# Value items of odd units in slots 3, 7 and 11, between the groups of value matmuls, in a two-layer attention kernel

## The reference

```python
Q = (q_in @ wq + bq).reshape(Bq, Sq, H, HD)
Kp = (k_in @ wk + bk).reshape(Bq, Sk, H, HD)
V = (v_in @ wv + bv).reshape(Bq, Sk, H, HD)
scores = jnp.einsum('bqhd,bkhd->bhqk', Q, Kp) / jnp.sqrt(jnp.float32(HD))
a = jax.nn.softmax(scores, axis=-1)
o = jnp.einsum('bhqk,bkhd->bqhd', a, V).reshape(Bq, Sq, Dm)
return o @ wo + bo
```

## Time and profile before

| what | value |
|---|---|
| median of 3 runs | 594.2 us (594.09 to 597.36) |
| profiled execution, its own time | 590.02 us |
| its span, first to last instruction | 588.2 us |
| mean granted TensorE clock | 0.937 |
| TensorE matmul busy | 518.5 us (88%) |
| VectorE busy | 431.1 us (73%) |
| ScalarE busy | 363.8 us (62%) |
| GpSimd busy | 205.7 us (35%) |
| L376, matmuls of the value items | 192 instructions for each layer's weights, 8 for each item |

### The profile page before, as it was taken

One profiled execution on the slowest core, in us unless ns is written; L12 is line 12 of the kernel. 1 busy time (PEld: TensorE's weight loads), 2 busy tenths in 40 slices (PEclk: granted clock), 3 DMA queues, 4 the chain that ended last, 5 costly groups with the idle time before them and its releaser, 6 DMA issues.

```text
span 588.2 us, 17011 instructions
## 1 busy us (share of the span) xinstructions
PE 518.5 (88%) x6536; PEld 378.8 (64%) x6536; DVE 431.1 (73%) x818; ACT 363.8 (62%) x716; POOL 205.7 (35%) x357
## 2 busy tenths in 40 slices
PE   6878779999999999998699993899999999999985
PEld 4756357676767767686467772467667676767763
DVE  7799978777777779876361126878989897978753
ACT  2556357777776776777334432476767667676663
POOL 8553123122130337353133002436547373530101
PEclk9789679999999999999869996699999999999998
DMA  6337478657747365465302310357373743528000
GB/s 162 102 116 210 156 194 250 171 183 180 205 144 196 130 193 153 137 183 175 95 2 86 91 37 15 101 157 218 141 185 125 190 151 108 168 69 228 12 3 17
DMA packets 41117, 79.99 MB, mean 136 GB/s; under 512 B 9327, under 2 KB 19247, under 8 KB 41055
## 3 DMA queue, kind: packets, MB, share of 16 engines
q1 hardware_dynamic: 41054, 79.16, 46.7%
HBM read 58.95 MB, written 20.13 MB: 134 GB/s over the span
## 4 chain that ended last, share of the span: by engine, by line
PE 57%; DVE 19%; ACT 8%; issue 8%; POOL 3%; DMA 3%; SPq 1%; ACTq 1%; POOLq 0%; DVEq 0%
PE bank L442 11%; PE bank L420 10%; PE bank L408 9%; PE bank L1302 5%; PE bank L376 4%; PE bank L370 4%; PE bank L1291 4%; DVE mx L609 4%; PE bank L364 3%; DVE qfix L601 2%; ACT qfix L539 2%; DMA k_scratch<-kparts 2%; PE bank L382 2%; ACT scratch L562 2%; DVE weights L1490 1%
## 5 line engine op out<-in xcount | busy, mean ns | idle before, releaser
L609 DVE TENSOR_REDUCE mx<-bank 112x1 f32<-112x500 f32 x384 | 245.3, 673 | 45.8 <-PE bank L408 42.8
L562 ACT ACTIVATE scratch<-bank 125x448 f32<-125x448 f32 x384 | 203.6, 548 | 111.9 <-PE bank L420 110.1
L408 PE MATMUL bank<-krep,qfix 96*112 96x500 bf16 (+1 forms) x384 | 153.6, 410 | 5.3 <-DVE mx L609 2.7
L420 PEld LDWEIGHTS bank<-qfix,krep 99*128 99x128 bf16 (+1 forms) x1536 | 107.6, 101 | 73.3 <-issue 26.0
L420 PE MATMUL bank<-qfix,krep 99*128 99x112 bf16 (+1 forms) x1536 | 140.1, 215 | 15.3 <-ACT qfix L539 10.1
L442 PE MATMUL bank<-scratch,v 125*32 125x112 f32 x3072 | 94.0, 262 | 0.0
L442 PEld LDWEIGHTS bank<-scratch,v 125*32 125x32 f32 x3072 | 70.2, 109 | 9.2 <-ACT scratch L562 0.6
L735 POOL TENSOR_TENSOR oT<-comb,rec 128x56 f32<-128x56 f32 x32 | 10.0, 312 | 175.0 <-DVE rec L631 175.0
L408 PEld LDWEIGHTS bank<-krep,qfix 96*112 96x112 bf16 (+1 forms) x384 | 51.5, 136 | 29.3 <-issue 18.6
L724 POOL TENSOR_TENSOR kparts<-k_rest,kparts 128x500 bf16<-128x500 f32 x48 | 54.3, 1139 | 43.1 <-ACT kparts L546 42.8
L1302 PEld LDWEIGHTS bank<-scratch 128*112 128x112 f32 x256 | 32.7, 182 | 16.0 <-issue 10.7
(11 more groups left out here) (172 smaller groups left out, 706.3 us busy)
## 6 DMA issues: line engine op xcount, KB each, us to landing
krep<-k_scratch SPq DMA_DIRECT2D x192, 187.5 KB, 4.0
k_scratch<-kparts SPq DMA_DIRECT2D x16, 1125.0 KB, 4.5
ctx_tile<-in_ctx SPq DMA_DIRECT2D x16, 750.0 KB
scratch<-in_L_xattn_e_w SPq DMA_DIRECT2D x16, 256.0 KB, 3.1
Q<-q_scratch SPq DMA_DIRECT2D x12, 168.0 KB, 3.1
q_scratch<-scratch SPq DMA_DIRECT2D x6, 168.0 KB, 2.5
Q<-q_scratch SPq DMA_DIRECT2D x12, 56.0 KB, 2.3
k_rest<-in_selq SPq DMA_DIRECT2D x1, 576.0 KB, 11.1
```

The costliest lines, as they stand in the source:

```text
L408: nc.tensor.matmul(row_bank(v, c, lead)[0:PQ, 0:KB], qfix[0:KR[l], slot, p * PQ:(p + 1) * PQ], krep[0:KR[l], slot, p, n * KB:(n + 1) * KB] ...
L420: ins = nc.tensor.matmul(SCORES[c % 2][:, p * PQ:(p + 1) * PQ], krep[0:KS[l], slot, p, c * KP:c * KP + 128], qfix[0:KS[l], slot, p * PQ:(p ...
L562: nc.scalar.activation(P[:, p_slot(s_, slot), :], SCORES[slot % 2][0:KP, 0:UQ], ACT.Exp, scale=SCALE).then_inc(z["exp_ok"], 1)
L609: nc.vector.tensor_reduce(mx[:, par, c // NKB, c % NKB:c % NKB + 1], row_bank(v, c, lead)[0:PQ, 0:KB], AX.X, ALU.max).then_inc(z["row_max" ...
```

## The change

The table of items gives odd units their V items in slots 3, 7 and 11 in place of 1, 5 and 8. As V2 now stands behind M, the list that tells an item which one was two places before it, `before` in `pe_attend`, starts the later passes with M and V2 in that order.

```diff
         STEP_ITEMS = [
...
-            {1: [("V", 1, 0)], 4: [("D", -1)], 5: [("V", 1, 1)], 8: [("V", 1, 2)], 10: [("M", 1)]},
+            {3: [("V", 1, 0)], 4: [("D", -1)], 7: [("V", 1, 1)], 10: [("M", 1)], 11: [("V", 1, 2)]},
...
-            {1: [("V", 2, 0)], 4: [("D", -1)], 5: [("V", 2, 1)], 8: [("V", 2, 2)], 10: [("M", 1)],
+            {3: [("V", 2, 0)], 4: [("D", -1)], 7: [("V", 2, 1)], 10: [("M", 1)], 11: [("V", 2, 2)],
              13: [("D", 0)]},
...
-                before = [("V", 2 * j, 2, 0, l), ("D", -1, 0, 3, l) if begins(j) else ("M", 4 * j, 0, 0, l)]
+                before = [("V", 2 * j, 2, 0, l), ("D", -1, 0, 3, l)] if begins(j) else \
+                    [("M", 4 * j, 0, 0, l), ("V", 2 * j, 2, 0, l)]
```

## The result

| | before | changed |
|---|---|---|
| median of 18 runs each | 593.95 us | 596.75 us |
| ratio to before, 95% interval | | 1.0063 (1.0041 to 1.0084) |
| profiled execution, its own time | 590.02 us | 594.52 us |
| its span | 588.2 us | 592.7 us |

The forecast was 597.2 us on a base of 594.2, +0.5%. The changed kernel is slower by 0.6%, clear of no change in 18 runs, and by less than the 1% that the prediction took as the least that could be told from no change. (The quotient of the two medians alone is 1.0047, inside the interval.)

A forecast was written before the change was run, and what follows sets the result against it. TensorE was taken to bound ordinary odd units, with a blocked VectorE copy lengthening six others. Terms 0.0 + 4.4 - 1.2 - 0.15 summed to +3.0 us, giving 597.2 us on a base of 594.2; range 588.5 to 600.0.

The forecast's parts named there:

- (a): Six ordinary layer 0 odd units followed by T items: M 0.80 us earlier, T1 later behind it, net 0.0.
- (b): Six long odd units: qfix copy still blocked by GpSimd's multiplication, M unmoved, T1 later by 0.73 us each, +4.4.
- (c): Layer 1 units 11 and 13, whose successors have no T items: -0.6 us each, -1.2.
- (d): Last unit of layer 0: V2 fills TensorE's wait for an exponential ahead of the last score matmuls, -0.15 us.
- rival C: Ordinary odd units: GpSimd's five steps gate M, so it comes no earlier; +9.4 us, 603.6 us; chance 0.08.
- Rival A: Long odd units: qfix copy gets in before GpSimd's multiplication, freeing them; sum -4.2 us, 590.0 us; chance 0.27.
- Rival B: Start of even units: T1 doesn't wait for ScalarE's copy of V2; sum +0.4 us, 594.6 us; chance 0.15.

The follow-up runs named there:

- e1: The changed kernel with V2 back in slot 8, ahead of M, V0 and V1 staying in slots 3 and 7; ratio to the kernel before 1.0009.
- e2: The kernel before with only V2 moved, from slot 8 to slot 11 behind M; ratio to the kernel before 1.0102.
- e3: The changed kernel with the three T items of even units one slot later (1, 2, 3); ratio to the kernel before 1.0104.
- e4: The kernel before with VectorE's copy of queries into qfix in slot 4 in place of 5; ratio to the kernel before 0.9892.
- e6: The kernel before with V0 of odd units in slot 0 in place of 1; ratio to the kernel before 0.9785.

## Why the prediction was right

The forecast had the sign, the size (+0.5% against +0.6%) and the mechanism: V2 leaves a place where its 0.87 us cost little, ahead of M, and enters one where nothing hides it. e1 shows that it is V2 and not the other two, and the changed kernel's own rows show where.

By terms, from the lengths between M items in the profiled executions (changed less before):

| term | forecast | measured |
|---|---|---|
| (a) six ordinary units with T behind them | 0.0 | about +1.8: four pairs +0.22 to +0.25, unit 13 and its successor +0.56, unit 1 and its successor +0.27 (+1.43 less the 1.16 by which the transfer's wait grew) |
| (b) six long units | +4.4 | +3.75: five pairs of layer 1 +4.10 together, unit 11 of layer 0 -0.35 |
| (c) two units without T behind them | -1.2 | -0.72 |
| (d) last unit of layer 0 | -0.15 | +0.02 (M of unit 14 to the first M of layer 1) |
| sum | +3.0 | about +4.8 |

The parts that are in no term: 0.15 us up to the M of layer 0's first unit, -1.35 in layer 1's first unit at its other clock, -0.27 behind the last M, and the transfer's 1.16. With them, the span's +4.5 is complete.

That the totals lie so near is in part luck: the ordinary units cost 1.8 us where I had nothing, (c) won 0.5 us less, and the one copy that got in first gave 1.1 us back.

(a) and (c) were mis-sized by one step: "Ahead of M, an ordinary unit gets shorter by 0.87 - 0.07 = 0.80". It measured 0.59 in unit 5 and 0.52 to 0.61 in the others but unit 13 of layer 0. The 0.07 is there in units 5 and 9 (0.50 between the first two score matmuls) and is 0.14 in the others (0.57), and I had not followed the exponentials through the slots that are bare now, so that the score matmuls of slot 9 wait 0.17 us for that of slot 7. e2 shows the same in a purer form. In unit 13 of layer 0 M itself then waits 0.18 us for GpSimd's steps, a trace of rival C, and there the odd unit became only 0.28 shorter. In (d) the wait of 0.15 is gone, but with V2 out of slot 8 the score matmuls at 281.74 and 285.09 wait 0.21 and 0.44 us for exponentials; that unit is 0.19 longer up to its last sums. Behind M the forecast was T1 at M + 3.07, measured 3.06, with 0.05 us more for T1 itself, whose weight load waits with it.

(b) was right in five units, where the even unit grew by 0.77 to 0.86 in place of 0.73, and wrong in the sixth. Rival A was real: the 0.11 to 0.20 us by which I had GpSimd first became 0.10 to 0.12, and in unit 11 of layer 0 the copy won. Freed, this unit's M came 1.19 us earlier, for which rival A had 1.2. Had all six gone so, the measured terms would sum to about -1.0; the starts of the two outcomes lie within 0.02 us.

Rival B (T1 follows without a wait) was wrong: T1 waits the 0.22 us that I had, and e3, which takes this wait away, puts another of the same size behind it. Rival C did not decide ordinary units: but for unit 13 their M has no wait in front of it.

By the rule of the Trainium skill that the prediction weighed ("SBUF — State Buffer", section "Who interferes with whom": whichever is issued first holds the shared port pair to the end, and the other is blocked), the traces now show both outcomes: the copy blocked, 2.77 us long, and the copy unhindered with the multiplication 0.17 us longer.

## What to carry to other kernels

An item that fills an engine's order is worth what waits behind its place, not what it weighs: look for the slot where the engine waits for something that the item doesn't feed (here 0.63 us ahead of a unit's first scores, 2% in all with the copies that got in first, of which I had foreseen none), and leave items where they stand in the shadow of another engine's stall. Moving an item past the point where two engines meet takes it out of one stretch's slack and can put its full length into the next (here 0.84 us for an item of 0.87). And when two engines want the same thing within 0.1 or 0.2 us of each other, take the tie away first (e4: one slot, 1.1%), since any other change of the order can tip it.

## What was not expected of the hardware

How sharp the tie is. The GpSimd multiplication is recorded as starting first in every one of these pairs, and yet it doesn't always block VectorE's copy. Copies begun 0.10 us (changed kernel, unit 11) and 0.09 to 0.12 us (e6, all six long units) after it ran first, in 0.21 or 0.22 us, and the multiplications took 2.91 to 2.93 us in place of 2.75. Copies begun 0.11 and 0.12 us after it, in the five units of layer 1 of the changed kernel, were held for 2.77 or 2.78 us. So the moment from which the multiplication blocks seems to lie about 0.1 us behind its recorded start, and at 0.11 and 0.12 us the recorded distance no longer tells the two outcomes apart. What decides there stays open.
